# State-space sums as accumulated outputs of ScalarE, and the residual of the last two stages added on VectorE

## What is computed

```
x = LN(x + ssm(x));  x = LN(x + cross_attention(x, ctx));  x = LN(x + gelu_ffn(x))
x = LN(x + causal_attention(x));  x = LN(x + single_head(x, ctx));  x = LN(x + ffn(x))
```

## Time and profile before

| | before |
|---|---|
| median of 3 runs | 3473.65 us (3470.51 to 3475.12) |
| the profiled execution | 3474.93 us, its span 3473.2 us |
| state-space phase | 0 to 655 us, clock 0.90: PE busy 517.55, DVE 573.10, ACT 412.73, POOL 468.09 us |
| single-head phase | 2664 to 2800.4 us, clock 0.93: PE 108.50, DVE 47.45, ACT 62.99, POOL 11.19 |
| last phase | 2800.4 to 3473.2 us, clock 0.98: PE 646.83, DVE 102.94, ACT 203.38, POOL 0 |

### The profile page before, as it was taken

How to read it: one execution, slowest core, us unless ns; L and a number is a source line. 1 busy time by engine, 2 the same in 40 slices (tenths; PEclk the granted TensorE clock), 3 DMA queues, 4 the chain that set the end, 5 groups by cost and what they waited for, 6 DMA issues and landing times. The chain is left out here.

```text
span 3473.2 us, 44194 instructions
## 1 busy us (share of the span) xinstructions
PE 3122.7 (90%) x12438; PEld 1669.8 (48%) x12438; DVE 1767.0 (51%) x2623; ACT 1993.0 (57%) x3736; POOL 1151.4 (33%) x954
## 2 busy tenths in 40 slices
PE   5888888799999999957679999999998879999999
PEld 2333333477777777722234444444444634444443
DVE  5999999455555555589934333333333311111110
ACT  4676676266666666545657777777775523333333
POOL 4778778222222222256623333333332000000000
PEclk8999999799999999988889999999999979999999
DMA  3545544100000000011100000000001300000000
GB/s 99 165 141 159 159 140 141 47 18 22 16 22 18 20 22 16 14 45 48 42 22 14 14 18 14 14 14 14 14 17 43 124 27 19 21 21 21 18 18 15
DMA packets 104264, 159.17 MB, mean 46 GB/s; under 512 B 11904, under 2 KB 44560, under 8 KB 104208
## 3 DMA queue, kind: packets, MB, share of 16 engines
q1 hardware_dynamic: 97872, 144.89, 12.4%
q10 hardware_dynamic: 6336, 13.60, 1.3%
HBM read 85.77 MB, written 4.72 MB: 26 GB/s over the span
## 5 line engine op out<-in xcount | busy, mean ns | idle before, releaser
L1355 POOL TENSOR_TENSOR d_pr<-d_pr,d_keep 128x512 f32<-128x512 f32 x256 | 320.4, 1273 | 566.7 <-ACT d_pr L1513 566.7
L770 POOL TENSOR_TENSOR b_pn<-b_e,b_inv 128x616 f32<-128x616 f32 x128 | 161.3, 1260 | 605.4 <-DVE b_inv L951 605.4
L256 POOL TENSOR_TENSOR a_bx<-a_bcopy,a_drive_u 128x512 f32<-128x512 f32 x256 | 319.9, 1270 | 17.2 <-DVE a_state L523 11.9
L523 DVE TENSOR_TENSOR_SCAN a_state<-a_decay,a_bx 128x512 f32<-128x512 f32 x256 | 311.2, 1215 | 2.4 <-POOL a_bx L256 1.9
L276 PE MATMUL a_py<-a_prod,consts 128*128 128x512 f32 x512 | 293.2, 657 | 2.3 <-DVE a_t L503 1.2
L1908 PE MATMUL f_ph<-f_hb,wb 128*128 128x512 f32 x512 | 232.8, 599 | 6.3 <-ACT f_hb L1943 6.3
L447 ACT ACTIVATE a_decay<-a_delta,neg_a 128x508 f32<-128x508 f32 x256 | 174.1, 682 | 102.1 <-DVE a_state L523 101.9
L1908 PE MATMUL f_ph<-f_ha,wb 128*128 128x512 f32 x512 | 229.0, 596 | 2.3 <-DVE f_ha L1972 2.3
L926 DVE TENSOR_REDUCE b_peak<-b_pscore 128x8 f32<-128x616 f32 x128 | 102.3, 799 | 216.4 <-PE b_pscore L807 216.4
L876 ACT ACTIVATE b_yy<-b_py,y_bias 128x154 f32<-128x154 f32 x512 | 169.4, 382 | 67.6 <-PE b_py L816 67.5
L1577 DVE TENSOR_SCALAR d_ln<-d_pn 128x512 f32<-128x512 f32 (+1 forms) x160 | 101.8, 636 | 197.5 <-PE d_pn L1408 197.5
(11 more groups left out here) (283 smaller groups left out, 6570.4 us busy)
## 6 DMA issues: line engine op xcount, KB each, us to landing
a_bcopy<-rows SPq DMA_DIRECT2D x256, 256.0 KB, 3.5
wb<-in_wb ACTq DMA_DIRECT2D x14, 480.0 KB, 3.7
a_xf<-in_x SPq DMA_DIRECT2D x16, 256.0 KB, 3.8
a_xt<-in_x ACTq DMA_DIRECT2D x16, 256.0 KB, 2.9
x<-a_xo SPq DMA_DIRECT2D x16, 256.0 KB, 2.3
b_xf<-x SPq DMA_DIRECT2D x32, 128.0 KB, 2.0
b_xt<-x SPq DMA_DIRECT2D x32, 128.0 KB, 2.0
x<-b_xo SPq DMA_DIRECT2D x32, 128.0 KB, 2.0
```

The source lines that it names most:

```text
L256: gp.tensor_tensor(bx[:, k % 4, :], bcopy[:, k % 4, :], drive_u[:, p, :], ALU.mult).then_inc(*bxt.step("bx"))
L523: V.tensor_tensor_scan(state[:, j % 2, :], decay[j % 2][:], bx[:, j % 4, :], 0.0, ALU.mult, ALU.add).then_inc(*vs.step("scan"))
L770: gp.tensor_tensor(heads(pn[:, j % 2, :]), heads(e[:, j % 2, :]), over(inv[:, j % 2, :], CTX), ALU.mult).then_inc(*pnt.step("n"))
L1355: gp.tensor_tensor(half, half, keep[:].unsqueeze(1).to_broadcast([128, QP, SEQ]), ALU.mult).then_inc(*gmt.step(f"m{odd}"))
```

## The change

In the state-space phase ACT writes the square sq, the convolution's output conv and the square csq as four instructions of 128 columns each, one per sequence, and each gives the sum over its 128 columns as an accumulated output into a column of `small` (slots 1, 4 and 5 of that tile; slot 5 is used for csq alone). The three VectorE reduces are dropped. PE's variance product waits for sq, DVE's csub for conv, and ACT's clnv for csq.

In the single-head and the last phase the centring product of the residual is dropped. DVE adds the residual instead, in a new tile t1 (in the single-head phase with the bias), ACT squares t1 and DVE multiplies t1 by the reciprocal deviation. The bank po is free when this sum is done. SP's load of xt no longer waits for PE's output of g-1 but for its own earlier load and the sum of g-2. The residual itself is not centred any more.

```diff
-        vf = tr("vf", "sum sub ssum csum csub cssum clip")
+        vf = tr("vf", "sum sub csub clip")
@@ ssm_phase, front_pe
-                        pe.wait_ge(*vf.at("ssum", g))
+                        pe.wait_ge(*sf.at("sq", g))
@@ ssm_phase, front_act, k == 1, 7, 9, 10
-                        A(f2[:], f1[:], ACT.Square).then_inc(*sf.step("sq"))
+                        for b in range(NB):
+                            op = A(b4(f2[:])[:, b, :], b4(f1[:])[:, b, :], ACT.Square, accum_out=small[:, 1, b:b + 1])
+                        op.then_inc(*sf.step("sq"))
...
-                        A(conv[:], pf[:], ACT.Identity, bias=W["conv_b"]).then_inc(*sf.step("conv"))
+                        for b in range(NB):
+                            op = A(b4(conv[:])[:, b, :], b4(pf[:])[:, b, :], ACT.Identity, bias=W["conv_b"],
+                                   accum_out=small[:, 4, b:b + 1])
+                        op.then_inc(*sf.step("conv"))
...
-                        A(f2[:], f1[:], ACT.Square).then_inc(*sf.step("csq"))
+                        for b in range(NB):
+                            op = A(b4(f2[:])[:, b, :], b4(f1[:])[:, b, :], ACT.Square, accum_out=small[:, 5, b:b + 1])
+                        op.then_inc(*sf.step("csq"))
...
-                        act.wait_ge(*vf.at("cssum", g))
+                        act.wait_ge(*sf.at("csq", g))
@@ ssm_phase, front_dve, k == 2, 9, 10
-                        V.tensor_reduce(small[:, 1, :], b4(f2[:]), AX, ALU.add).then_inc(*vf.step("ssum"))
...
-                        V.tensor_reduce(small[:, 4, :], b4(conv[:]), AX, ALU.add).then_inc(*vf.step("csum"))
...
-                        V.tensor_reduce(small[:, 5, :], b4(f2[:]), AX, ALU.add).then_inc(*vf.step("cssum"))
@@ single_phase, sync (the same in ffn_phase)
-                            sp.wait_ge(*peo.at("out", g - 1))
+                            if begun(g - 2):
+                                both = [(load_t, 16 * g), vo.at("sum", g - 2)]
+                                wait_all(sp, *(both if p == 0 else reversed(both)))
+                            else:
+                                sp.wait_ge(load_t, 16 * g)
@@ single_phase, tensor
-                        pe.wait_ge(load_t, 16 * g)
                         pe.wait_ge(*sm.at("p", g - 1))
                         if begun(g - 2):
-                            pe.wait_ge(*vo.at("out", g - 2))
-                        mm(po[:], S["center"], xt[:, q, :], start=True, stop=False, skip_group_check=True)
+                            pe.wait_ge(*vo.at("sum", g - 2))
...
@@ single_phase, scalar
-                        act.wait_ge(*peo.at("out", g - 1))
-                        A(t2[:], po[:], ACT.Square, bias=S["c_bo"][:, 1:2]).then_inc(*so.step("sq"))
+                        act.wait_ge(*vo.at("sum", g - 1))
+                        A(t2[:], t1[:], ACT.Square).then_inc(*so.step("sq"))
@@ single_phase, vector: ahead of the main part of the step, and the output at its end
+                        dve.wait_ge(*peo.at("out", g - 1))
+                        dve.wait_ge(load_t, 16 * g)
...
+                        V.scalar_tensor_tensor(out=t1[:], in0=po[:], scalar=S["c_bo"][:, 1:2], in1=xt[:, q, :],
+                                               op0=ALU.add, op1=ALU.add).then_inc(*vo.step("sum"))
...
-                        V.scalar_tensor_tensor(out=xo[:, q, :], in0=po[:], scalar=S["c_bo"][:, 1:2], in1=t3[:],
-                                               op0=ALU.add, op1=ALU.mult).then_inc(*vo.step("out"))
+                        V.tensor_tensor(xo[:, q, :], t1[:], t3[:], ALU.mult).then_inc(*vo.step("out"))
@@ ffn_phase, tensor, slot 0 (scalar: the square reads t1 after vo "sum", as above)
-                            mm(po[:], S["center"], xt[:, q, :], start=True, stop=False)
@@ ffn_phase, vector, slot 0 (after peo "out" and load_t), and slot 3
+                            V.tensor_tensor(t1[:], po[:], xt[:, q, :], ALU.add).then_inc(*vo.step("sum"))
...
-                            V.tensor_tensor(xo[:, q, :], po[:], t3[:], ALU.mult).then_inc(*vo.step("out"))
+                            V.tensor_tensor(xo[:, q, :], t1[:], t3[:], ALU.mult).then_inc(*vo.step("out"))
```

More of the change, by code:

```diff
@@ L495, in front_dve @@
                     if k == 10:
-                        dve.wait_ge(*sf.at("csq", g))
-                        V.tensor_reduce(small[:, 5, :], b4(f2[:]), AX, ALU.add).then_inc(*vf.step("cssum"))
                         V.tensor_scalar(b4(pf[:]), h0, -40.0, None, ALU.max).then_inc(*vf.step("clip"))
@@ L1630, in single_phase @@
         small = sb("small", [128, 3, NB])
+        t1 = sb("t1", [128, N])
         t2 = sb("t2", [128, N])
@@ L1653, in single_phase @@
         so = tr("so", "sq ln rstd")
-        vo = tr("vo", "out")
+        vo = tr("vo", "sum out")
         def heads(ap):
@@ L1782, in step @@
                     q = 1 - p
+                    if tail:
+                        dve.wait_ge(*peo.at("out", g - 1))
+                        dve.wait_ge(load_t, 16 * g)
+                        if begun(g - 2):
+                            dve.wait_ge(*vo.at("out", g - 2))
+                        V.scalar_tensor_tensor(out=t1[:], in0=po[:], scalar=S["c_bo"][:, 1:2], in1=xt[:, q, :],
+                                               op0=ALU.add, op1=ALU.add).then_inc(*vo.step("sum"))
                     if main:
@@ L1911, in step @@
                             pe.wait_ge(*sm.at("gelu", SLOTS * g - 1))
-                            pe.wait_ge(load_t, 16 * g)
                             if begun(g - 2):
-                                pe.wait_ge(*vo.at("out", g - 2))
-                            mm(po[:], S["center"], xt[:, q, :], start=True, stop=False)
+                                pe.wait_ge(*vo.at("sum", g - 2))
                             for i in range(FC):
-                                op = mm(po[:], W["f3"][:, 128 * i:128 * (i + 1)], hc[:, i, :], start=False, stop=i == FC - 1)
+                                op = mm(po[:], W["f3"][:, 128 * i:128 * (i + 1)], hc[:, i, :], start=i == 0, stop=i == FC - 1)
                             op.then_inc(*peo.step("out"))
@@ L1944, in step @@
                         if tail and k == 0:
-                            act.wait_ge(*peo.at("out", g - 1))
-                            A(t2[:], po[:], ACT.Square).then_inc(*so.step("sq"))
+                            act.wait_ge(*vo.at("sum", g - 1))
+                            A(t2[:], t1[:], ACT.Square).then_inc(*so.step("sq"))
                         if tail and k == 2:
@@ L1973, in step @@
                                                    in1=pab[1][:], op0=ALU.mult, op1=ALU.mult).then_inc(*vf.step("prod"))
+                        if tail and k == 0:
+                            dve.wait_ge(*peo.at("out", g - 1))
+                            dve.wait_ge(load_t, 16 * g)
+                            if begun(g - 2):
+                                dve.wait_ge(*vo.at("out", g - 2))
+                            V.tensor_tensor(t1[:], po[:], xt[:, q, :], ALU.add).then_inc(*vo.step("sum"))
                         if tail and k == 3:
```

5 lines of the change are left out of this document (1 added, 4 removed).

## The result

The median after is **3426.49 us** (four runs, 3424.75 to 3427.96) against 3473.61 before: a ratio of 0.9867, interval [0.9855, 0.9879], 47 us faster. The span went from 3473.2 to 3426.2 us.

| stretch | before | after | difference | forecast |
|---|---|---|---|---|
| start to last a_xo (state-space) | 653.4 | 636.6 | -16.8 | +16.4 |
| last a_xo to last d_xo (touched by nothing but what a neighbour leaves) | 2008.9 | 2004.9 | -4.0 | 0 |
| last d_xo to last e_xo (single-head) | 134.6 | 122.0 | -12.6 | -18.8 |
| last e_xo to the end (last phase) | 676.3 | 662.7 | -13.6 | -13.1 |

A forecast was written before the change was run, and what follows sets the result against it. Bounds: a ring through ScalarE (state-space), TensorE awaiting bank po's late read (single-head), TensorE itself (last stage). 3474.93 - 18.8 - 13.1 + 16.4 = 3459.4, taken as 3458 on the median's scale; range 3431 to 3475.

The forecast's parts named there:

- the term 124r: State-space stage: total cost of accumulated outputs, within 124r - 13.4, which gave +16.4 us at r = 0.24.
- r: State-space stage: time an accumulated output adds to one ScalarE piece, taken as 0.24 us, ends 0 and 0.48.
- Accumulating is nearly free: Rival for the state-space stage: r below 0.1, stage gains 1 to 13 us, kernel at 3428 to 3441; chance 0.10.
- The slower rival: State-space stage: accumulator read by its own operation that waits for the pipe; r above 0.42, 3488 at 0.48; chance 0.15.
- ssum's 0.6 is lost in the 8 groups of 13 in which L503 waits for TensorE anyway: State-space stage: dropping this reduce gains only in the other 5 groups, 0.23 us on the mean.
- 8r - 0.86: State-space stage: mean change in us per group, over the 14 groups with this work beside their scans in full.
- 8r - 0.63: State-space stage, conv to e1: shift of e1 in us, added work 0.55 + 8r less ScalarE's slack of 1.18.
- hide behind ScalarE's longer bursts: State-space stage: dropping the csum and cssum reduces gains little, because ScalarE's longer work covers them.
- The ring through ScalarE: State-space stage: loop from L512 through scans, csub, csq, cz, e1 and rstd2 back to L512, setting the group.
- The last phase: Last stage: TensorE loses L1915, 0.86 us in 16 groups, less 0.7 at the end: -13.1 us.
- The single-head term: Single-head stage: new ring of 6.27 us instead of 7.52, 1.25 less in 15 periods: -18.8 us.
- the softmax chain binds: Rival for the single-head stage: costlier hand-overs, period 6.6, gain 14 instead of 18.8, kernel at 3463; chance 0.12.

The follow-up runs named there:

- e1: Only the three accumulated sums on ScalarE, residuals as in the kernel before; 3451.05 us, ratio 0.9945.
- e8: The whole change plus a VectorE reduce of a constant tile, read by nobody, where ssum stood; 3443.33 us, ratio 0.9910.
- e12: The kernel before plus three unread TensorE products (the filler) at the end of each state-space group; 3463.35 us, ratio 0.9977.
- e13: The whole change with csq's four accumulating squares made twice, 1.16 us more on ScalarE between conv and e1; 3447.45 us, ratio 0.9933.
- e3: Only the residual edit of the last phase, against the kernel before; 3459.65 us, ratio 0.9959.
- e5: The kernel before with only sq accumulated on ScalarE and ssum dropped; conv and csq keep their reduces; 3463.07 us, ratio 0.9972.
- e6: The kernel before with only conv and csq accumulated on ScalarE; 3468.15 us, ratio 0.9987.
- e11: The whole change plus three unread TensorE products (the filler) at the end of each state-space group; 3422.04 us, ratio 0.9864.
- e10: e8 plus three unread TensorE products (the filler) at the end of each state-space group; 3439.00 us, ratio 0.9913.
- e4: The whole change with the single-head phase's VectorE sum moved behind the subtraction and ScalarE's square behind the Exp; 3419.25 us, ratio 0.9845.

## Why the prediction was wrong

**The price of the accumulated output (the term 124r) was mis-sized.** r was taken as 0.24 from ScalarE's operations on four columns at 0.20, "a little" added for the drain. Rows of the change show 0.35 and 0.30 a piece from start to start, which leaves 0.09 to 0.12 for r against the estimated pieces. That makes 124 x 0.14 = 17 us for the mean of 0.10. The rival "Accumulating is nearly free" was nearest on the price, and 0.10 was too small a chance for it, but its times, 3428 to 3441, lie above the result too: even r = 0 does not bring the forecast's sum down to 3426, so other steps failed as well. The slower rival had the mechanism right, a reading instruction of its own, but it overlaps its neighbours. The fault was to add the price of a lone small operation to a piece in a full queue. The Trainium skill, "ScalarE: Activation LUTs", section What ACT_TABLE_LOAD costs, names no price for this output and so gave r = 0; the trace stands between, nearer to that. The same page's Rules for kernel authors would have additions on VectorE; here the sums on ScalarE made the kernel 22.6 us faster (e1), so for a sum that rides on an operation made anyway the measurement decides against the rule.

**"ssum's 0.6 is lost in the 8 groups of 13 in which L503 waits for TensorE anyway" failed, and it is the larger error in kind.** I took TensorE's lateness in those groups as a fixed thing. It is not: the reduce L488 stands on VectorE just where TensorE starts again after its pause, and with a reduce there TensorE stays at half clock for 6.5 us, without it mostly for 3.5, and L503's wait goes with it (e8 against the change). With the clock held high the reduce costs its 0.59 in every group (e12 against the change), and without the filler 1.42 (e8, the group shown). Per group the forecast's 8r - 0.86 with the measured r is -0.06; measured is 35.91 - 37.39 = -1.48. Of this gap of 1.42, 0.36 is the reduce in the other 8 groups (0.59 - 0.23), 0.65 the half clock (0.91 - 0.26), of which 0.41 is the second place that the forecast had no term for, and 0.41 the stretch from conv to e1. The 13 groups make -19.2 us; the time ahead of the first L512 and the last two groups give 2.4 back, which makes the -16.8.

**The term 8r - 0.63 for conv to e1 had the wrong sign at the measured r.** It gives +0.17. In the group shown the stretch did grow by 0.18, but that agreement is luck: the slack was read in one group of before, and this stretch varies there from 7.12 to 8.36. At clock 1.00 it is 8.28 before and 8.04 after, 0.24 less. That csum and cssum "hide behind ScalarE's longer bursts" is therefore not quite so: with the sums on ScalarE csub comes 0.71 earlier after conv (2.05 for 2.76). The edit that lets the variance product wait for sq and not for ssum gives nothing: L503 to conv is 6.03 with and without it.

**What held.** The ring through ScalarE: e13 shows that work put between conv and e1 arrives in full. The last phase was right: -13.6 for -13.1, 0.81 to 0.86 a group, and -14.0 alone (e3).

**The single-head term was right in mechanism and too large by 6 us.** Link by link the ring is the forecast's; it is 0.45 longer. Of that some 0.27 is the hand-over of po: 1.10 was read where ScalarE takes a bank that TensorE has just filled, and VectorE takes it after 1.34 to 1.40 in most groups. The subtraction to the reduce is 1.00 instead of 0.96, the reduce to e_pn 0.86 to 0.94 instead of 0.85, transposes to scores 0.50 to 0.60 instead of 0.50. The rival "the softmax chain binds" had 6.6 and is nearest. Kernels with the old single-head phase show 7.33 (e1, e3, e5) as well as 7.52 (before; 7.53 in e6), so of the -12.6 some 3 us may be scatter of the kernel before.

The sum with the terms as measured is 3474.9 - 17 - 13 - 14 = 3431 on the scale of the profiled execution; the -4 in the phases that no edit touched makes up the rest (the profiled execution after took 3427.96), and since that stretch differs by as much between other kernels that have it unchanged (2008.9 us before, 2003 to 2011 in the experiments, from the last a_xo to the last d_xo), it is scatter.

**Open:** why TensorE's stretch at half clock is in some groups 3.5 and in others 6.5 to 7 us, why the second place falls to half clock in some groups and not in others with the same pause of 1.79 us (e12 has both), why reduces of csum and cssum lead to it and the pieces do not beyond the shorter pause of 1.20, and why the filler kept the clock up in the first place in all groups of e12 and e11 but only in some of e10. That e6 and e8 both settle at 37.55 us is no riddle: both have the pieces of conv and csq and one reduce where ssum stood, and their parts are the same (10.37, 6.76, 7.78, 12.64). e13's 37.54 is made of other parts (9.35, 6.45, 9.09, 12.64).

## What to carry to other kernels

A wait that looks like cover for an instruction ("lost, since TensorE is late anyway") must be asked what it depends on: where the late engine is at half clock after a pause just before, the instruction may be part of the cause, and taking it away can gain more than its own time. Read a slack in several groups, not in one, and know whether the profiled execution was a short or a long one of its kernel. Price a small instruction in a full queue by the distance from start to start, never by the duration of a lone one; a sum over columns is cheap on ScalarE where ScalarE writes those columns anyway. When a ring through several engines is the bound, list the second-latest wait of each engine before moving one link: e4 gained only until the next one.

## What the runs showed of the hardware

The accumulated output is a separate instruction of 0.19 to 0.22 us that overlaps both neighbours; a piece of 128 columns with it takes 0.35 (Identity) and 0.30 us (Square) from start to start, some 0.09 to 0.12 above the estimate without it. A bank that TensorE fills reached VectorE 1.34 to 1.40 us after the start of its eight passes in most groups, where ScalarE had it after 1.10. After pauses of TensorE of 2.3 to 3 us in a group of 37 its granted clock was 0.50 for 3.5 to 7 us; three unread products in that place (2.84 us of TensorE) kept it at 1.00 there and made the unchanged kernel 9 us faster. In 4 of 13 groups it also fell to 0.50 for some 3.4 us after a pause of 1.79 us.
